# Masked attention beside a routed mixture: score banks, mask order and the place of the next chunk's products

## The reference, cut to what matters

```python
xn = layernorm(x)
out = x + attention(xn) + mixture(xn)

# attention: 16 heads of 16; 4 see all earlier tokens, 12 see the last 64 only
q, k, v = split(xn @ w_qkv + b_qkv)
mask_g = diff < 0
mask_l = (diff < 0) | (diff > 64)              # diff = query - key
ctx = softmax(where(mask, -inf, q @ k.T / 4)) @ v
attention = ctx @ w_out + b_out

# mixture: twice (forward, and inverse with weight alpha), 8 experts of rank 64
Q, K = xn @ W_Q.T, xn @ W_K.T
xV, yW = Q @ V[k], K @ W[k]
weights = softmax(gelu(Q @ router_w1.T + b1) @ router_w2.T + b2 + expert_bias)
branch = ((xV * cumsum(yW) * weights[k]) @ U[k] + weights @ b) / (position + 1)
mixture = (fwd + alpha * inv) @ W_O.T
```

## Time and profile before

| | us |
|---|---|
| median of 3 runs (lowest to highest) | 1487.91 (1486.12 to 1490.52) |
| the profiled execution | 1491.34 |
| its span, first to last instruction | 1489.6 |
| TensorE busy | 1379.5 (93%) |
| VectorE busy | 989.5 (66%) |
| ScalarE busy | 776.1 (52%) |
| GpSimd busy | 586.5 (39%) |
| mean granted TensorE clock, share of full speed | 0.989 |

### The profile page before, as it was taken

One profiled execution on the slowest core, in us unless ns is written; L12 is line 12 of the kernel. 1 busy time (PEld: TensorE's weight loads), 2 busy tenths in 40 slices (PEclk: granted clock), 3 DMA queues, 4 the chain that ended last, 5 costly groups with the idle time before them and its releaser, 6 DMA issues.

```text
span 1489.6 us, 35980 instructions
## 1 busy us (share of the span) xinstructions
PE 1379.5 (93%) x14481; PEld 1035.7 (70%) x14481; DVE 989.5 (66%) x2082; ACT 776.1 (52%) x1368; POOL 586.5 (39%) x663
## 2 busy tenths in 40 slices
PE   5978999999999999999999999999999999999996
PEld 4567685777758677586856778587775868667773
DVE  6667777567756777557875677566875578656661
ACT  2434537455464735645374554646356453755544
POOL 1025343453514444253433525144452534335341
PEclk9999999999999999999999999999999999999998
DMA  8430625326062541616353171624516153431610
GB/s 189 102 94 11 168 79 127 105 65 174 25 175 70 121 126 49 166 32 151 96 123 107 40 196 30 158 87 107 141 42 163 44 146 100 118 109 42 172 40 15
DMA packets 166614, 152.88 MB, mean 103 GB/s; under 512 B 37809, under 2 KB 149808, under 8 KB 166448
## 3 DMA queue, kind: packets, MB, share of 16 engines
q1 hardware_dynamic: 166448, 150.59, 38.8%
HBM read 108.57 MB, written 35.65 MB: 97 GB/s over the span
## 4 chain that ended last, share of the span: by engine, by line
PE 62%; DVE 15%; ACT 8%; issue 6%; DMA 4%; POOL 2%; SPq 1%; ACTq 0%; POOLq 0%; DVEq 0%
PE PS L676 30%; PE PS L787 11%; PE PS L821 4%; DVE rest L1193 3%; PE PS L880 3%; ACT HE L1063 3%; PE PS L807 3%; PE PS L909 3%; PE PS L898 2%; PE PS L963 2%; DMA weights_d<-weights_t 2%; DVE area L1198 2%; DVE area L1196 2%; ACT HE L1055 2%; ACT PS L1048 1%
## 5 line engine op out<-in xcount | busy, mean ns | idle before, releaser
L1504 POOL TENSOR_TENSOR PL<-prod,PH 128x512 fp32r<-128x512 f32 x128 | 164.7, 1287 | 201.3 <-ACT PH L1037 201.3
L676 PE MATMUL PS<-XH,WH 128*128 128x512 f32 x512 | 218.6, 427 | 21.7 <-ACT prod L1027 10.3
L1037 ACT ACTIVATE PH<-prod 128x512 fp32r<-128x512 f32 x128 | 80.8, 632 | 268.8 <-DVE prod L1305 252.8
L1499 POOL TENSOR_TENSOR prod<-prod,rest 128x512 f32<-128x512 f32 x96 | 124.8, 1303 | 242.9 <-DMA rest<-weights_d 166.6
L1229 DVE TENSOR_REDUCE block_peak<-PS 128x4 f32<-128x512 f32 x288 | 179.8, 685 | 48.0 <-PE PS L821 47.9
L676 PE MATMUL PS<-XH,WL 128*128 128x512 f32 x512 | 204.1, 399 | 0.0
L676 PE MATMUL PS<-XL,WH 128*128 128x512 f32 x512 | 203.6, 398 | 0.0
L1482 POOL TENSOR_SCALAR_AFFINE_SELECT HE<-HE 128x256 f32<-128x256 f32 x128 | 51.2, 406 | 364.2 <-ACT HE L1063 360.6
L1063 ACT ACTIVATE HE<-PS 128x512 f32<-128x512 f32 (+1 forms) x320 | 159.9, 553 | 33.5 <-PE PS L880 30.5
L1305 DVE TENSOR_TENSOR prod<-PS,prod 128x512 f32<-128x512 f32 x128 | 87.8, 686 | 97.3 <-PE PS L676 84.5
L676 PEld LDWEIGHTS PS<-XH,WH 128*128 128x128 f32 x512 | 97.1, 190 | 63.2 <-ACT prod L1027 16.8
(11 more groups left out here) (186 smaller groups left out, 3064.6 us busy)
## 6 DMA issues: line engine op xcount, KB each, us to landing
parts_d<-area SPq DMA_DIRECT2D x32, 768.0 KB, 5.0
area<-parts_d SPq DMA_DIRECT2D x128, 192.0 KB, 7.9
rest<-weights_d SPq DMA_DIRECT2D x192, 128.0 KB, 3.0
area<-parts_d SPq DMA_DIRECT2D x32, 576.0 KB, 7.8
tok<-in_L_attn_x_dram SPq DMA_DIRECT2D x16, 512.0 KB, 6.2
xt<-in_L_attn_x_dram SPq DMA_DIRECT2D x16, 512.0 KB, 4.1
wide<-weights_d SPq DMA_DIRECT2D x64, 128.0 KB, 3.0
out_dram<-xt SPq DMA_DIRECT2D x16, 512.0 KB, 3.8
```

The lines of the kernel that those rows point to most:

```text
L676: ins = e.matmul(ps, a, b, start=first and k == 0, stop=last and k == n - 1, skip_group_check=True)
L1037: e.activation(PH[:, h, :], prod[:, j % 3, :], ACT.Copy).then_inc(phi)
L1499: e.tensor_tensor(prod[:, j % 3, :], prod[:, j % 3, :], wide[j % WIDE], ALU.mult).then_inc(weighed)
L1504: e.tensor_tensor(PL[:, j % 2, :], prod[:, j % 3, :], PH[:, j % 2, :].bitcast(F32), ALU.subtract).then_inc(plo)
```

## The change

- The local scores' banks: pair 0 is always in bank 5, pair 1 in bank 6 and bank 4 by turns. The mask of unit n + 1 is written ahead of unit n's exponentials, and the first unit's mask, which was a product, is written as the others are, before the last two expert groups. All three local groups have their context in bank 7 (the second had bank 4).
- The peaks are woven into the expert groups but the last two, so into two groups fewer.
- The routing weights are stored with one DMA of all 128 partitions, instead of four of eight partitions each. The spreading DMAs read each row in two halves.
- In the global stage the next chunk's second and third `x` come between the blocks, the first `values` before the last context block and the second `values` behind it; the three `weigh` come at the end.
- In chunk 0 the next `x` products come earlier, and the whole norm of chunk 1 runs ahead of the first product. The order of `open` and the following `x` is now in chunk 0 as in the others. In the last chunk the first `finish` goes to the middle of the global stage.

```diff
@@ -112,7 +112,7 @@
     CTX_AT = {1: (0, 0), 2: (0, 1), 3: (1, 0), 0: (1, 1)}
 
     def ctx_bank(grp):
-        return 7 if grp % 2 else 4
+        return 7 if grp else 4
 
 
 
@@ -235,15 +235,15 @@
     def local_groups(ch):
 
         units = [(grp, half) for grp in range(1, 1 + NL // 4) for half in range(2)]
-        scores = [(ch, grp, half, pair, score_use()) for grp, half in units for pair in range(2)]
+        scores = [(ch, grp, half, pair, f"bank{6 - 2 * (n % 2) if pair else 5}") for n, (grp, half) in enumerate(units) for pair in range(2)]
+        masks = [[(add_seed, bank, "lscore", *key)] for *key, bank in scores[1::2]]
         order = []
         for n, (grp, half) in enumerate(units):
-            order.append([(add_lscore, *scores[2 * n]), (add_lscore, *scores[2 * n + 1])])
-            if n + 1 < len(units):
-                order[-1].append((add_seed, scores[2 * n + 3][4], "lscore", *scores[2 * n + 3][:4]))
+            order.append(masks[n + 1] if n + 1 < len(units) else [])
+            order[-1] = order[-1] + [(add_lscore, *scores[2 * n]), (add_lscore, *scores[2 * n + 1])]
             if n:
                 order[-1].append((add_lav, ch, *units[n - 1]))
-        return order
+        return order, masks[0]
 
     def global_groups(ch):
         order = []
@@ -258,7 +258,7 @@
 
         order = []
         for j in range(2 * KB):
-            if j < 2 * KB - 1 and (j > 1 or not ch):
+            if 1 < j < 2 * KB - 1:
                 order.append([(add_x, ch, j + 1, part) for part in range(2)] + [(add_weigh, ch, j + 1)])
             order.append([(add_c, ch, j, part) for part in range(2)] if j else [])
             order[-1].append((add_product, ch, j))
@@ -320,8 +320,6 @@
         gpeaks[2].append((add_rows, ch, 0))
         gpeaks[-1].append((add, "found", ch, 1))
         order += gpeaks
-        if ch == 0:
-            add_norm(1, order)
         blocks = range(0, len(order), PEAKS)
         joined = lambda groups, n: [stage for group in groups[n:n + PEAKS] for stage in group]
         return [joined(order, n) + joined(masks, n + PEAKS) for n in blocks]
@@ -379,6 +377,9 @@
     add_weigh(0, 0)
     for part in range(2):
         add_c(0, 0, part)
+    for part in range(2):
+        add_x(0, 1, part)
+    add_weigh(0, 1)
 
     for ch in range(CHUNKS):
         nxt = ch + 1 < CHUNKS
@@ -387,9 +388,18 @@
         split = len(experts) - (0 if nxt else 4)
         if ch:
             experts[1].append((add_finish, ch - 1, 1))
-            experts[2], experts[3] = experts[3], experts[2]
-        run(experts[0] + peaks[0])
-        weave(experts[1:split], peaks[1:])
+        experts[2], experts[3] = experts[3], experts[2]
+        if ch:
+            run(experts[0] + peaks[0])
+        else:
+            run(peaks[0] + [(add_x, 0, 2, part) for part in range(2)] + [(add_weigh, 0, 2)] + peaks.pop(1))
+            for n in range(len(NORM)):
+                add("norm", 1, n)
+            run(experts[0])
+        weave(experts[1:split - 2], peaks[1:])
+        locals_, first_mask = local_groups(ch)
+        for group in [first_mask] + experts[split - 2:split]:
+            run(group)
         if ch:
             add_residual(ch)
 
@@ -402,7 +412,7 @@
                 side[-1].append((add, "load", ch + 2))
         else:
             side = [[(add_rows, ch, 1)]] + experts[split:] + [last_mix]
-        weave(local_groups(ch), side)
+        weave(locals_, side)
         add_lav(ch, NL // 4, 1)
         add("cturn", ch, 0)
         if not nxt:
@@ -414,33 +424,34 @@
                 add_hidden(ch + 1, j)
 
         order = global_groups(ch)
-        side = []
         if nxt:
-            first_x, first_c = ([(add, ch + 1, 0, part) for part in range(2)] for add in (add_x, add_c))
-            run(first_x + order[0] + first_c)
+            x0, x1, x2 = ([(add_x, ch + 1, j, part) for part in range(2)] for j in range(3))
+            run(x0 + order[0] + [(add_c, ch + 1, 0, part) for part in range(2)])
             add("logits", ch + 1, uses=["bank7"])
             add("chigh", ch, 0)
+            if ch + 2 < CHUNKS:
+                add_norm(ch + 2, order[1:-2])
+            steps = 2 + 3 * (ch % NC)
+            last = len(order) // 2 - 1
+
+            order[1] += [(add_gates, ch + 1), (add, "crest", ch, 0)]
+            for n, other in ((0, [(add_gate_parts, ch + 1)]), (steps // 2, x1), (steps, x2), (steps + steps // 2, [(add_finish, ch, 0)]),
+                             (last - 1, [(add_values, ch + 1, 0)])):
+                order[2 * n + 2] += other
             order = order[1:]
-            if ch + 2 < CHUNKS:
-                add_norm(ch + 2, order)
-            side = [[(add_gates, ch + 1)], [(add_gate_parts, ch + 1)]] + [[]] * (2 * (ch % NC))
-            side += [[(add_values, ch + 1, 0)], [(add_values, ch + 1, 1)]]
-            side[0].append((add, "crest", ch, 0))
         else:
             add("crest", ch, 0)
-        side.append([(add_finish, ch, 0)])
-        weave(order, side)
+            order[len(order) // 2].append((add_finish, ch, 0))
+        for group in order:
+            run(group)
         if nxt:
+            add_values(ch + 1, 1)
             add("stacks", ch + 1, "global")
-        if nxt:
-            add_weigh(ch + 1, 0)
-            run([(add_x, ch + 1, 1, part) for part in range(2)])
-            add_weigh(ch + 1, 1)
         add("cturn", ch, 1)
         add("chigh", ch, 1)
         if nxt:
-            run([(add_x, ch + 1, 2, part) for part in range(2)])
-            add_weigh(ch + 1, 2)
+            for j in range(WIDE):
+                add_weigh(ch + 1, j)
         add("crest", ch, 1)
     add_finish(CHUNKS - 1, 1)
 
@@ -529,7 +540,7 @@
 
         parts_d = nc.dram_tensor("parts_d", (2, D, 3, C), BF16, kind="Internal").ap()
         peak_d = [nc.dram_tensor(f"peak_d_{n}", (3 * k, C), BF16, kind="Internal").ap() for n, k in (("local", NL), ("global", NG))]
-        weights_d = nc.dram_tensor("weights_d", (2 * KE, C), F32, kind="Internal").ap()
+        weights_d = nc.dram_tensor("weights_d", (P, HALF), F32, kind="Internal").ap()
         rows_d = nc.dram_tensor("rows_d", (3, 2 * KE, C), BF16, kind="Internal").ap()
         xr = x.rearrange("n (c t p) d -> n c p t d", c=NC, t=T)
         outr = out.rearrange("n (c t p) d -> n c p t d", c=NC, t=T)
@@ -1288,7 +1299,7 @@
                     q.wait_step()
                     q.step(e.tensor_tensor(w_2, w_1, gate_b[:, 1], ALU.subtract))
                     q.wait_step()
-                    q.wait_ge(weights_out, 16 * 4 * ch)
+                    q.wait_ge(weights_out, 16 * ch)
                     q.wait_ge(rows_cast, ch)
                     e.transpose(weights_t[:, :], wslots[:, :, :].rearrange("p b k -> p (b k)")).then_inc(weights_turned)
                     q.wait_ge(weights_turned, ch + 1)
@@ -1624,10 +1635,7 @@
                     q.wait_ge(weights_turned, ch + 1)
                     for i in range(WIDE):
                         q.wait_ge(wide_in[i], 16 * 2 * (use(f"wide{i}", "wide", ch, i) - 1))
-                    for w in range(2):
-                        for h in range(2):
-                            row = 32 * (2 * w + h)
-                            e.dma_start(weights_d[KE * w:KE * (w + 1), h * HALF:(h + 1) * HALF], weights_t[row:row + KE, :]).then_inc(weights_out, 16)
+                    e.dma_start(weights_d, weights_t[:, :]).then_inc(weights_out, 16)
                     q.wait_ge(rows_cast, ch + 1)
                     q.wait_ge(rows_in, 16 * 3 * ch)
                     for w in range(2):
@@ -1646,7 +1654,7 @@
 
                 elif kind == "wide":
                     ch, j = key
-                    q.wait_ge(weights_out, 16 * 4 * (ch + 1))
+                    q.wait_ge(weights_out, 16 * (ch + 1))
                     if j >= WIDE:
                         q.wait_ge(weighed, nth("weigh", ch, j - WIDE))
                     elif j == 2:
@@ -1656,8 +1664,11 @@
                         q.wait_ge(clo, DB * (ch + 1))
                         if ch == 0:
                             q.wait_ge(bias_in, 16 * 15)
+
+                    by_half = weights_d[2 * 32 * (j // KB):2 * 32 * (j // KB + 1), :].rearrange("(h e) t -> e h t", h=2)
                     for k in range(2):
-                        e.dma_start(wide[j % WIDE][R * k:R * (k + 1), :], weights_d[2 * j + k:2 * j + k + 1, :].to_broadcast([R, C])).then_inc(wide_in[j % WIDE], 16)
+                        n = 2 * (j % KB) + k
+                        e.dma_start(wide[j % WIDE][R * k:R * (k + 1), :].rearrange("p (h t) -> p h t", h=2), by_half[n:n + 1].to_broadcast([R, 2, HALF])).then_inc(wide_in[j % WIDE], 16)
 
                 elif kind == "finish" and key[1] == 1:
                     ch, k = key
```

## The result

The changed kernel takes 1514.95 us (median of 4 runs, 1511.12 to 1519.04), the one before 1487.01 (4 runs beside them, 1483.97 to 1490.52): 1.0187 of it, 95% interval 1.0152 to 1.0223, so 1.9% or 27.9 us slower. The prediction said 1495.0 within 1477 to 1506: slower, but by a quarter of what was measured. The profiled execution took 1511.12 us, its span is 1509.4. From that product to the end the changed execution takes 24.3 us more.

The account below looks back on a forecast made before the run. TensorE's own work was taken as the bound (busy 75.6 of 79.1 and 90.1 of 95.1 us), with DMA setting even chunks' ends. Terms +12.0, -1.4, -1, -2.5 sum to +7.1 us: 1495.0 against the median, range 1477 to 1506.

Parts of the forecast that it names:

- start: Chunk 0's new order: first product delayed by the next norm, later TensorE waits gone; -1 us, from -5 to +5.
- eight even chunks: Next chunk's first `c`, released by the DMA chain, comes later by 0.7 + 0.3 + 0.5: 1.5 us each, +12.0.
- seven odd chunks: Peaks' seeds +0.8, local stage +0.05, global stage -1.05 us in each odd chunk; -1.4 in all.
- end: Last chunk: first finish no longer in front of the global blocks, a mask wait gone, denser peaks about 1; -2.5 us.
- Local stage, even chunks: Shared bank 7 makes context products wait for transposes, the third group's by +1.9; 0.7 us passes to DMA, 1.0 to hidden layer.
- Local stage, odd chunks: Peaks ending a block earlier win about 1.1 us, 0.7 down to VectorE's `parts`; hidden layer starts where it did: +0.05.
- a rival at 0.10: TensorE's wait before an odd chunk's first `c` drops the clock: 1.7 us, eight times, +13, 1508 us; chance 0.10.
- Peaks: Odd chunks' second block of peaks waits for VectorE's reductions at two seeds, +0.8 us each chunk; even chunks keep their spacing.
- Weights: One 128 KB store lands +0.3 us later behind the stacks' loads; broadcasts in 1 KB halves take +0.5, between 0 and +1.1.
- Global stage: Next chunk's products among the blocks remove TensorE waits: -1.05 us in odd chunks, nothing won in even ones, held by DMA.
- Chunk 0 and the last chunk: Norm delays chunk 0's first product about 5 us, later waits go: -1 in all; last chunk's moved finish: -2.5 us.
- a sign of being wrong: The prediction called itself wrong if, among other signs, chunk 0's order moves more than 5 us.

## Why the prediction was wrong

The direction was right, the size was not. The prediction counts by place, and so can the two profiled executions, from the very first `c` product on (chunk 0 counts as even from its local stage on, in front of it as start):

| | forecast, us | measured, us |
|---|---|---|
| eight even chunks | +12.0 | +17.8 |
| seven odd chunks | -1.4 | +7.0 |
| start | -1 | +0.2 |
| end | -2.5 | -0.7 |
| sum | +7.1 | +24.3 |

The 3.6 us from there to 27.9 lie between these two executions and the medians and have no place. Step by step:

**Local stage, even chunks: right in kind, mis-sized.** It named the transpose of the third group behind the keys' `parts`, put the context product 1.9 us later and let 0.7 (DMA) and 1.0 (hidden layer) of it through. Measured are 2.1 us later (16.70 after the stage's start for 14.57) and 1.25 at the global stage. The second group's context product was stepped at +0.3 and comes 0.32 later (7.63 after the stage's start for 7.31). TensorE's idle time before it, named as near 0.5 us, is 0.97, since TensorE arrives there sooner. From the local stage to the next first `c` chunk 6 loses 1.6 us, for a forecast of 1.5.

**Local stage, odd chunks: the step that failed.** It said +0.05, because the peaks' earlier end would pay for the later contexts. Measured is +0.66 (26.94 us from the local to the global stage, for 26.28). The peaks did pay: with them squeezed and the local part undone, the global stage starts 25.3 us after the local one. With the local part it starts at 26.94, 1.65 later, and 1.5 of that are the twelve products at half clock. The clock was a rival at 0.10, priced at 1.7 us a chunk, but looked for at one place only, the first `c` of an odd chunk. There the changed kernel waits 1.0 to 1.2 us in five of the seven, and its clock did not fall once. The waits that the forecast itself created in the local stage were not put to that test. In nine of fifteen local stages the clock fell at them, and the run with filled waits showed, on the kernel with the bank alone, that the clock, not only the standing, was lost. Nine times 1.5 us are some 13 us, an estimate from these rows: without them the changed kernel would stand near 1502, inside the range. No run took the clock's part alone out of the changed kernel.

**Peaks: right in odd chunks, a term put at nothing in even ones.** The seeds at the second block stand 0.18 twice, as forecast from the earlier trace rows (0.8 from start to start), and chunk 7 takes 0.77 us more to its local stage (38.32 for 37.55). "Even chunks keep their spacing" was priced at nothing; they lose 0.6 us each at the seventh `c`, behind `found` in VectorE's queue. Against both stands a gain in chunk 0. As a whole the edit gives 3 us, where the forecast had it cost 5.6 and return nearly 8 in the local stages of odd chunks.

**Weights: right.** +0.8 an even chunk, 6.4 in all, were forecast, 4.5 measured alone, part of it perhaps the clock. The store lands no sooner behind the stacks (+0.1 for +0.3), and the broadcasts take 0.4 to 0.5 more, as taken. By the Trainium skill, page "DMA: Bandwidth & Descriptors", section "Rules for kernel authors", the one large store should have come sooner; the trace does not agree, with 6.15 us for 6.05.

**Global stage: over-estimated.** Odd chunks were to gain 1.05 and gain 0.37, a second miss of the size of the local one: the waits went from the end of the stage, but the weighing moved behind them and `c` waits 0.52 us for it. In even chunks the wait of over 1 us before `c` is there (1.05).

**Chunk 0 and the last chunk: the sum near, the account wrong.** -1 was forecast in front. The norm was to delay the first `c` by 5 us; it delays it by 6.5 (17.4 us after the very first `c` for 10.9). TensorE stands for 9.27 us, and 10 us run at half clock (TensorE's timeline of the changed kernel, and the stretch):

```profile
96.94 0.79 PE L687 MATMUL PS<-CH,WH 128*128 128x512 f32 x1 [9.27 <-DVE prod L1316]
```

```profile
92.00:102.10 10.10, 5.16 (x39) 3.95 (x40) 6.49 (x24) 1.83 (x3) 2.02 (x3) 0.50 0.28 69
```

The later waits of the chunk go, as forecast, and the local stage starts 50.8 us after the very first `c`, for 50.6 before. But the squeezed peaks alone bring it to 46.3. So the order is not paid by what it was to save: beside the peaks it costs 6 to 7 us, more than the 5 that the prediction named as a sign of being wrong. The working named the new gap and its clock and gave them no price of their own. The last chunk gains 0.7 us, not 2.5.

By parts instead of places, as the runs give it: local part +20, chunk 0's order +7, weights +4, peaks and global order -3, together +28, for a forecast of +7. The mix of parts matters: the local part costs 44 us alone and 20 beside the others. The likely reason is that there the first mask stands ahead of the copy that it waits for in the local part alone; no run moved that mask by itself.

## What to carry to other kernels

When a change gives an accumulator's PSUM bank to several groups in turn, look at what stands in the draining engine's queue between two of them; here six operations made one renamed bank 23 to 27 us dear. Put every wait that a forecast creates on TensorE, also those that seem covered, to the question of the clock, and price it by rows at both levels. And try the parts one by one: of the five here one gained (the peaks, most when kept out of the even chunks), one did no harm (the global order), and these two without the rest beat both kernels.

## What the runs showed of the hardware

**A cast of VectorE stands while GpSimd works.** VectorE's and GpSimd's timelines of the changed kernel, at the last peaks of chunk 6:

```profile
661.39 1.20 DVE L1261 CAST peak_t_global<-peak_rest 128x128 bf16<-128x128 f32 x1
662.63 0.29 DVE L1263 TENSOR_TENSOR peak_t_global<-peak_rest,peak_t_global 128x128 bf16<-128x128 f32 x1
662.84 0.68 DVE L1316 TENSOR_TENSOR prod<-PS,prod 128x512 f32<-128x512 f32 x1
```

```profile
661.14 1.37 POOL L1510 TENSOR_TENSOR prod<-prod,rest 128x512 f32<-128x512 f32 x1 [1.24 <-ACT prod L1038]
```

The cast takes 1.20 us and ends when GpSimd's product does; the same cast took 0.23 in chunk 6 before. It lies in front of the product that the seventh `c` waits for, so it is the likely source of the 0.6 us that squeezing costs each even chunk (1.20 us there too with the peaks alone moved; in odd chunks it takes 0.23 and this `c` does not wait); no run took it away alone. The larger cast of `parts` takes 0.43 alone and 1.47 beside GpSimd (678.00 above). Its mean rose from 521 to 672 ns:

```profile
L1207 DVE CAST area<-rest 128x512 bf16<-128x512 f32 x64 | 43.0, 672 | 2.2
```

Other operations of VectorE stand beside GpSimd too, and the change moves them out of its way: the last of the three on `parts` (L1198, now L1209) fell from 919 to 723 ns on the mean, and VectorE's busy time as a whole from 989.5 to 975.1 us. So the casts alone do not make VectorE slower here; the order decides which of them stands.

The Trainium skill, page "SBUF — State Buffer", section "Who interferes with whom", says that VectorE's casts can use a port pair that it shares with GpSimd, and that the second to start blocks until the first is done. The trace agrees.

**Repeating work can pay.** Some 2.3 us of useless products in each local stage (an estimate: 72 products take 2.28 us where 16 take 0.64, and 80 were added) made a kernel 7 to 11 us faster, as its granted clock rose from 0.975 to 0.991.
